# A graph network's edge passes: single rows fetched from ScalarE's DMA queue instead of SyncE's

## The chip, the cores and the metric

The kernel runs on one core of one Trainium2 chip. A core has five engines with instruction streams of their own: TensorE (PE), VectorE (DVE), ScalarE (ACT), GpSimd (POOL) and SyncE (SP), which computes nothing and issues DMAs. Sixteen DMA engines move the data. The metric is the device time of one execution in microseconds (us), lower is better; the kernel before takes 6624.49 us (median of 3 runs, 6611.32 to 6628.42).

## The reference, cut to what matters

Two graph layers over 12500 nodes of 128 features and 200000 edges, sorted by their destination. The first is attention with 8 heads, the second a plain sum over the neighbours:

```python
q, k, v = (h @ W + b for each of Wq, Wk, Wv)       # 12500 x 128
e = sum(q[dst] * k[src]) / 4                       # per edge and head
p = exp(e - segment_max(e, dst)[dst]); z = segment_sum(p, dst)
agg = segment_sum((p / z[dst]) * v[src], dst)
...                                                # projection, norm, MLP
neigh = segment_sum(h2[src], dst)                  # second layer
out = x + relu((h2 + neigh) @ W1 + b1) @ W2 + b2
```

(The self loops of the first layer, the norms and the residuals are left out here.) The costly part is `k[src]`, `v[src]` and `h2[src]`: 200000 rows at addresses that only the edge list tells.

## The kernel before, in words

The work goes in stages, named by the letters of the functions: A (node projections, search of where each node's edges start), B (first edge pass, from about 400 to 3300 us of the span), C (nodes: attention output and MLP), D (second edge pass, about 3640 to 6430 us) and E (nodes: last MLP).

**Edges.** Each of the 128 partitions owns 1568 consecutive edges, which are walked in 98 batches of 16 per partition. A running maximum and running sums go along the free axis by VectorE's scans, and each edge's running state is stored to memory.

**Gathers.** For a batch n, GpSimd issues 16 indirect DMAs (helper at L698), each of which fetches one row for each of the 128 partitions: keys and values (1 KB) into `kvb[n % 2]` in pass B, `h2` rows (512 B) into `rows[n % 2]` in pass D. A buffer is free again once batch n - 2 is consumed (`weighed_s` in B, `rows_turned` in D).

**Single rows.** Both passes are written in octets of 8 batches (`octets`, L511): the first octet is peeled with fixed addresses, 11 are a hardware loop (`Fori`), and two batches are left. In every octet's slot 1, from the second octet on, the last of the 16 indirect DMAs is left out. Its 128 rows are instead fetched one by one by ordinary DMAs of one row each (`fetch`, DMAs at L594): SyncE loads their numbers into registers (`row_numbers`, two register loads at L587: a pointer, then the values), computes an address and issues the DMA. The 128 rows of the next octet are spread over the slots of this one: `ROWS_B` = 0, 8, then 20 in each of six slots; `ROWS_D` = 19, 19, then 18 in each of five, then 0. They land in `direct_kv` or `direct_h`, and one DMA of SyncE (L614 in B, L664 in D) copies them into their place in the batch's buffer (`direct_set` counts these copies).

**SyncE's other work.** In B, one load of 1 MB of queries per batch (L603, `q_in`), issued when ScalarE has turned earlier queries (`q_turned`), and one store of states of 1.15 MB (L580, after `stb_set`, counted in `states_out`). In D one store of sums per batch (L655, after `sums_set`, counted in `sums_out`). All of it is in one program order with the single rows.

**ScalarE in B** (`batch_b`, from L1115), per batch n: the gates and keep factors of batch n + 1 (L1097, L1099, L1103); wait for the queries and for VectorE's products (`prod_s`); keep the last query (L1126), turn the queries of batch n + 1 (two copies, L1108); exponential (L1131); then copies of top, z and both halves of the states into the buffer that is stored (L1135, L1138, two at L1142), each after VectorE's scan that makes it. **VectorE in B** multiplies and reduces (L1739, L1746), waits for the turned queries (L1680), scans for the maxima and sums (L1770 to L1832) and ends with the second scan of the states (L1810).

**ScalarE in D** (`slot_d`, from L1235), per batch: wait for the rows, turn them (L1247), indices and keep factors (L1248, L1231), wait for the store of two batches before (`sums_out`), then two copies of sums (L1254) after VectorE's two scans (L1994).

Of the kernel before, what the change touches and what calls it, by code (L numbers as in the profile page):

```python
# [55 lines left out]
EREST = E - EFULL * STEPS  # L56
OCTETS = BATCHES // 8
DIRECT_AT = 9 * B + B - 1
ROWS_B = (0, 8) + (20,) * 6
ROWS_D = (19, 19) + (18,) * 5 + (0,)  # L60
assert BATCHES == 8 * OCTETS + 2 and sum(ROWS_B) == P and sum(ROWS_D) == P
BPAIRS = BATCHES // 2
# [70 lines left out]
def build(nc, a, out):  # L133
    ctx = ExitStack()
    with ctx:
# [385 lines left out]
        def settle(eng):  # L521


            eng.sem_inc(turns, 1)

        def last_batch(n):
            return isinstance(n, int) and n == BATCHES - 1
# [8 lines left out]
        def _(sp):  # L536
# [42 lines left out]
                settle(sp)  # L579
                sp.dma_start(by_step(states0)[:, bass.ds(n * B, B), :], stb[k]).then_inc(states_out[k], 16)  # L580

            def row_numbers(o, by_slot, r):

                if not by_slot[r]:
                    return []
                p0 = sum(by_slot[0:r])
                return nc.values_load_multi_w_load_instructions(  # L587
                    direct_tab[bass.ds(o, 1), p0:p0 + by_slot[r]], engines=[mybir.EngineType.SP], min_val=0, max_val=N - 1,
                    skip_runtime_bounds_check_because="edges name nodes")[1]

            def fetch(to, tab, numbers, p0, done):

                for p, number in enumerate(numbers, p0):
                    sp.dma_start(to[p:p + 1, :], tab[bass.ds(number, 1), :]).then_inc(done, 16)  # L594

            def slot_b(o, r, first):

                n, k = o * 8 + r, r % 2
                if not last_batch(n):
                    if not (first and r == 0):  # L600
                        sp.wait_ge(q_turned, n * 2)
                        settle(sp)
                    sp.dma_start(qb[1 - k], q_rows[:, bass.ds(n * B + B, B), :]).then_inc(q_in[1 - k], 16)  # L603
                filling = not (isinstance(o, int) and o == OCTETS)
                numbers = row_numbers(o, ROWS_B, r) if filling else []
                p0, ahead = sum(ROWS_B[0:r]), len(numbers) // 2 if r > 1 else 0
                fetch(direct_kv, kv_tab, numbers[0:ahead], p0, direct_kv_in)
                if not (first and r == 0):
                    store_b(n - 1, 1 - k)
                if r == 0 and not first:  # L610
                    sp.wait_ge(direct_kv_in, o * 16 * P)
                    sp.wait_ge(weighed_s, n * 2)
                    settle(sp)
                    sp.dma_start(kvb[1][:, B - 1, :], direct_kv).then_inc(direct_set, 16)  # L614
                if r == 1 and not first and filling:
                    sp.wait_ge(direct_set, o * 16)
                    settle(sp)
                fetch(direct_kv, kv_tab, numbers[ahead:], p0 + ahead, direct_kv_in)
            sp.wait_ge(direct_listed, 16)
            octets(sp, slot_b)  # L620


# [25 lines left out]
            def slot_d(o, r, first):  # L648

                n, k = o * 8 + r, r % 2  # L650
                filling = not (isinstance(o, int) and o == OCTETS)
                numbers = row_numbers(o, ROWS_D, r) if filling else []
                sp.wait_ge(sums_set, n + 1)
                settle(sp)
                sp.dma_start(by_step(states1)[:, bass.ds(n * B, B), :], sums_b[k]).then_inc(sums_out[k], 16)  # L655
                if r == 0 and not first and filling:
                    sp.wait_ge(direct_set, (OCTETS + o) * 16)
                    settle(sp)
                fetch(direct_h, h2_tab, numbers, sum(ROWS_D[0:r]), direct_h_in)
                if r == 7:  # L660
                    sp.wait_ge(direct_h_in, o * 16 * P + 16 * P)
                    sp.wait_ge(rows_turned, n + 1)
                    settle(sp)
                    sp.dma_start(rows[1][:, B - 1, :], direct_h).then_inc(direct_set, 16)  # L664
# [364 lines left out]
        def _(act):  # L1029
# [66 lines left out]
            def gates(n, k):  # L1096
                nc.scalar.copy(keepz[k].rearrange("p (h t) -> p h t", h=NH)[:, :, 1:CW],  # L1097
                               keep[:, bass.ds(n * B, B)].unsqueeze(1).to_broadcast([P, NH, B])).then_inc(gates_set, 1)
                nc.scalar.copy(penb[k][:, 0:NH * CW].rearrange("p (h t) -> p h t", h=NH)[:, :, 1:CW],  # L1099
                               pen[:, bass.ds(n * B, B)].unsqueeze(1).to_broadcast([P, NH, B])).then_inc(gates_set, 1)  # L1100
# [12 lines left out]
            act.wait_ge(q_in[0], 16)  # L1113
            turn_queries(0)

            def batch_b(i, first):
                for k in range(2):
                    n = i * 2 + k
                    gates(n + 1, 1 - k)
                    keep_features(n + 1, 1 - k)  # L1120
                    if not last_batch(n):
                        act.wait_ge(q_in[1 - k], i * 16 + 16 + (16 if k else 0))
                        settle(act)
                        act.wait_ge(prod_s, (n + 1) * 2)
                        settle(act)
                        nc.scalar.copy(q_last, q_now[:, :, B - 1])  # L1126
                        act.drain()
                        turn_queries(1 - k)
                        nc.scalar.copy(idx[k][:], src_all[:, bass.ds((n + 2) * B, B)]).then_inc(idx_set, 1)
                    act.wait_ge(dif_s, n + 1)  # L1130
                    nc.scalar.activation(probs, dif.rearrange("p h t -> p (h t)"), ACT.Exp, scale=SCALE)\  # L1131
                        .then_inc(probs_s, 1)
                    if not first:
                        act.wait_ge(states_out[k], i * 16)
                    nc.scalar.copy(stb[k][:, :, SW:RW].rearrange("p b h -> p h b"), top[:, :, 1:CW])\  # L1135
                        .then_inc(top_out, 1)
                    act.wait_ge(zrun_s, n + 1)
                    nc.scalar.copy(stb[k][:, :, HID:SW].rearrange("p b h -> p h b"),  # L1138
                                   zrun[k].rearrange("p (h t) -> p h t", h=NH)[:, :, 1:CW]).then_inc(z_out, 1)
                    for half in range(2):  # L1140
                        act.wait_ge(state_s, n * 2 + half + 1)
                        done = nc.scalar.copy(stb[k][:, :, half * HF:(half + 1) * HF].rearrange("p b f -> p f b"),  # L1142
                                              sums_flat[:, half * HF * B:(half + 1) * HF * B].rearrange("p (f b) -> p f b", b=B))
                        if half == 0 and last_batch(n):
                            act.wait_ge(chunk_s, 4)
                            nc.scalar.activation(weight, masked, ACT.Exp, scale=SCALE).then_inc(chunk_act, 1)
                    done.then_inc(stb_set, 1)
            repeat(act, BPAIRS, batch_b, tail=1)


            act.wait_ge(chunk_ps, 2)
# [82 lines left out]
            def slot_d(o, r, first):  # L1234

                n, k = o * 8 + r, r % 2
                act.wait_ge(rows_in[k], o * (4 * BW - 16 * k) + r // 2 * BW + BW)
                if r == 1 and not first:
                    act.wait_ge(direct_set, (OCTETS + o) * 16)
                act.wait_ge(sum_s, n * 2 + 1)  # L1240
                if last_batch(n):
                    for half in range(2):
                        fs = slice(half * HF, (half + 1) * HF)
                        nc.scalar.copy(rows_now[:, fs, :], rows[k][:, :, fs].rearrange("p b f -> p f b"))\
                            .then_inc(rows_turned, 1)
                else:
                    nc.scalar.copy(rows_now, rows[k].rearrange("p b f -> p f b")).then_inc(rows_turned, 1)  # L1247
                    nc.scalar.copy(idx[k][:], src_all[:, bass.ds((n + 2) * B, B)]).then_inc(idx1_set, 1)  # L1248
                    keep1_features(n + 1, 1 - k)
                if not (first and r < 2):  # L1250
                    act.wait_ge(sums_out[k], o * 64 + r // 2 * 16)
                for half in range(2):
                    act.wait_ge(sum_s, n * 2 + half + 2)
                    done = nc.scalar.copy(sums_b[k][:, :, half * HF:(half + 1) * HF].rearrange("p b f -> p f b"),  # L1254
                                          run_sums[:, half * HF * B:(half + 1) * HF * B].rearrange("p (f b) -> p f b", b=B))
                done.then_inc(sums_set, 1)
            octets(act, slot_d)
            act.wait_ge(carry1_ps, 1)
            nc.scalar.copy(sameT, ps[:, 0, 0:P]).then_inc(sameT_s, 1)  # L1259
# [805 lines left out]
```

## Time and profile before

| | |
|---|---|
| median of 3 runs | 6624.49 us |
| span of the profiled execution | 6623.6 us |
| pass B, pass D (about) | 400 to 3300 us, 3640 to 6430 us |
| busy: POOL, DVE, ACT, PE | 3391.3, 2759.1, 2126.7, 517.3 us |
| DMA packets of SyncE's queue (q1) | 87088, 462.32 MB |
| DMA packets of ScalarE's queue (q10) | 14722, 13.70 MB |
| DMA packets of GpSimd's queue (q0) | 142272, 342.22 MB |

The span is the time from the first to the last instruction of one profiled execution. An engine's busy time counts its own work only: instructions for registers, branches, semaphores and the issuing of DMAs are not in it, and SyncE has no busy time at all. What an engine's sequencer does is seen in the rows whose engine name ends in q (SPq, ACTq). No engine is busy in more than about half of the span, so the order of the waits decides, and the chain of waits and the timeline have to be read.

### The profile page before, as it was taken

To read this page: it belongs to the slowest core of one execution; us is meant where nothing else is said; L and a number is where in the kernel's file an instruction comes from. 1 tells how busy PE (TensorE), PEld (TensorE's weight loads), DVE (VectorE), ACT (ScalarE), POOL (GpSimd) and SP (SyncE) were. 2 spreads that over 40 slices of the span, in tenths; PEclk is the share of its full clock that TensorE was granted. 3 is DMA by queue.
4 is the path that set the end of the run, shared out by engine and by line. 5 is a ranking of instruction groups with operands and counts; after the bars stand their busy time and mean duration, and the time that the engine had idled before them with its cause. 6 is when DMAs were issued, how large, how long until landed. Compare 5 with 4: busy or idle time off the path is not lost.

```text
span 6623.6 us, 31560 instructions
## 1 busy us (share of the span) xinstructions
PE 517.3 (8%) x2379; PEld 363.4 (5%) x2379; DVE 2759.1 (42%) x4388; ACT 2126.7 (32%) x2237; POOL 3391.3 (51%) x3586
## 2 busy tenths in 40 slices
PE   4400000000000000000076000000000000000006
PEld 2200000000000000000055000000000000000004
DVE  7556666566565566666665121112111111212112
ACT  3223333233333333333355332223232322323221
POOL 4665555455355455554353564645455454545534
PEclk8655555555555555555588555555555555555557
DMA  9954444444444444444344222222222222222223
GB/s 362 372 185 159 138 154 153 132 150 147 133 155 135 151 142 149 159 135 151 128 104 97 65 80 78 68 71 83 65 78 73 75 65 71 85 66 77 71 80 106
DMA packets 244283, 819.95 MB, mean 124 GB/s; under 512 B 70090, under 2 KB 103030, under 8 KB 193907
## 3 DMA queue, kind: packets, MB, share of 16 engines
q0 software_dynamic: 142272, 342.22, 19.0%
q1 hardware_dynamic: 87088, 462.32, 18.6%
q10 hardware_dynamic: 14722, 13.70, 0.6%
q14 instruction: 193, 1.57, 0.1%
q8 instruction: 8, 0.13, 0.0%
HBM read 455.00 MB, written 354.21 MB: 122 GB/s over the span
## 4 chain that ended last, share of the span: by engine, by line
SPq 47%; issue 35%; DVE 5%; PE 4%; DMA 3%; ACT 2%; POOL 2%; another core or an unknown queue 1%; POOLq 0%; ACTq 0%; DVEq 0%
SPq L594 31%; SPq L587 12%; DVE arena L1810 2%; DMA q_edges<-arena 2%; PE ps L1372 1%; PE ps L1361 1%; DVE ps L1687 1%; DMA arena<-q_edges 1%; SPq L580 1%; POOL q_edges L702 1%; SPq L655 1%; DVE ps L1793 1%; ACT ps L1108 1%; POOL arena L698 1%
## 5 line engine op out<-in xcount | busy, mean ns | idle before, releaser
L698 POOL DMA_INDIRECT arena<-kv_tab,idx x1556 | 1475.3, 948 | 1425.3 <-DVE ps L1793 926.2
L698 POOL DMA_INDIRECT arena<-h_tab,idx x1556 | 1472.0, 946 | 1302.4 <-ACT idx L1248 807.9
L1986 DVE SCALAR_TENSOR_TENSOR ps<-arena,keep,ps 128x128 f32<-128x128 f32 x97 | 42.5, 438 | 2297.5 <-ACT ps L1247 1947.1
L1254 ACT COPY arena<-arena 128x1024 f32<-128x1024 f32 x196 | 364.2, 1925 | 1714.0 <-DMA states<-arena 1651.4
L1142 ACT COPY arena<-arena 128x1024 f32<-128x1024 f32 x196 | 377.7, 1927 | 557.7 <-DVE arena L1810 474.0
L1687 DVE TENSOR_TENSOR_SCAN ps<-arena,ps 128x256 f32<-128x256 f32 (+2 forms) x584 | 502.6, 861 | 1.0 <-remote 0.9
L1680 DVE SCALAR_TENSOR_TENSOR ps<-arena,keep,ps 128x64 f32<-128x64 f32 x194 | 53.6, 276 | 1062.9 <-ACT ps L1108 1026.0
L1810 DVE TENSOR_TENSOR_SCAN arena<-arena,ps 128x1024 f32<-128x1024 f32 x196 | 443.4, 2262 | 6.0 <-remote 3.1
L1247 ACT COPY ps<-arena 128x2048 f32<-128x2048 f32 x97 | 346.8, 3576 | 284.7 <-DMA arena<-arena 153.3
L1994 DVE TENSOR_TENSOR_SCAN arena<-arena,ps 128x1024 f32<-128x1024 f32 x194 | 433.1, 2274 | 10.3 <-issue 0.5
L1108 ACT COPY ps<-arena 128x1024 f32<-128x1024 f32 x196 | 362.1, 1880 | 10.2 <-DMA arena<-q_edges 4.1
L1126 ACT COPY arena<-ps 128x128 f32<-128x128 f32 x97 | 25.5, 263 | 1009.4 <-DMA arena<-q_edges 996.5
L698 POOL DMA_INDIRECT arena<-states,node_idx x196 | 191.3, 976 | 152.8 <-issue 64.6
L1739 DVE TENSOR_TENSOR arena<-arena,ps 128x1024 f32<-128x1024 f32 x196 | 229.0, 1210 | 21.8 <-DMA arena<-kv_tab,idx 18.5
L1793 DVE TENSOR_TENSOR ps<-arena,ps 128x1024 f32<-128x1024 f32 x196 | 237.3, 1211 | 0.0
L1332 PE MATMUL ps<-arena,ones 128*128 128x512 f32 x4 | 3.8, 1101 | 2936.6 <-DVE arena L1713 2936.6
L1746 DVE TENSOR_REDUCE ps<-arena 128x64 f32<-128x1024 f32 x196 | 230.2, 1220 | 0.1
L1407 PE MATMUL ps<-arena 128*128 128x128 f32 x2 | 0.8, 501 | 2820.6 <-ACT arena L1259 2820.6
L1332 PEld LDWEIGHTS ps<-arena,ones 128*128 128x128 f32 x4 | 1.2, 324 | 2938.1 <-DVE arena L1713 2937.1
L1407 PEld LDWEIGHTS ps<-arena 128*128 128x128 f32 x2 | 0.5, 310 | 2820.8 <-ACT arena L1259 2820.8
L698 POOL DMA_INDIRECT arena<-dst_tab,idx x98 | 97.5, 995 | 103.1 <-DVE idx L1604 68.9
L702 POOL DMA_INDIRECT q_edges<-arena,start_i x98 | 101.6, 1037 | 39.7 <-issue 31.8
(252 smaller groups left out, 2510.0 us busy)
## 6 DMA issues: line engine op xcount, KB each, us to landing
states<-arena SPq DMA_DIRECT2D x98, 1152.0 KB
q_edges<-arena SPq DMA_DIRECT2D x98, 1024.0 KB
arena<-q_edges SPq DMA_DIRECT2D x98, 1024.0 KB
states<-arena SPq DMA_DIRECT2D x98, 1024.0 KB
arena<-kv_tab,idx POOLq DMA_INDIRECT x1556
arena<-h_tab,idx POOLq DMA_INDIRECT x1556
arena<-kv_tab SPq DMA_DIRECT2D x1536, 1.0 KB
arena<-h_tab SPq DMA_DIRECT2D x1536, 0.5 KB
```

What stands on the lines that cost most here:

```text
L587: return nc.values_load_multi_w_load_instructions(direct_tab[bass.ds(o, 1), p0:p0 + by_slot[r]], engines=[mybir.EngineType.SP], min_val=0, ...
L594: sp.dma_start(to[p:p + 1, :], tab[bass.ds(number, 1), :]).then_inc(done, 16)
L698: pool.indirect_dma_start(to, None, tab, bass.IndirectOffsetOnAxis(ap=at, axis=0)).then_inc(done, 16)
L1108: nc.scalar.copy(q_now[:, fs, :], qb[k][:, :, fs].rearrange("p b f -> p f b")).then_inc(q_turned, 1)
L1142: done = nc.scalar.copy(stb[k][:, :, half * HF:(half + 1) * HF].rearrange("p b f -> p f b"), sums_flat[:, half * HF * B:(half + 1) * HF * ...
L1247: nc.scalar.copy(rows_now, rows[k].rearrange("p b f -> p f b")).then_inc(rows_turned, 1)
L1254: done = nc.scalar.copy(sums_b[k][:, :, half * HF:(half + 1) * HF].rearrange("p b f -> p f b"), run_sums[:, half * HF * B:(half + 1) * HF ...
L1687: done = nc.vector.tensor_tensor_scan(part, keep_flat[n % 2][:, 0:(f1 - f0) * B], part, 0.0, ALU.mult, ALU.add)
L1746: nc.vector.tensor_reduce(score[:, :, 1 + b0:1 + b1].rearrange("p h t -> p t h"), kvb[n % 2][:, b0:b1, 0:HID].rearrange("p b (h d) -> p b ...
L1793: nc.vector.tensor_tensor(weighed.rearrange("p (h d) b -> p b h d", d=HD), values.rearrange("p b (h d) -> p b h d", d=HD), probs_h[:, half ...
L1810: nc.vector.tensor_tensor_scan(sums_flat[:, half * HF * B:(half + 1) * HF * B], keep_flat[n % 2], weighed_flat, 0.0, ALU.mult, ALU.add).th ...
L1994: nc.vector.tensor_tensor_scan(run_sums[:, part], keep1_flat[n % 2], rows_flat[:, part], 0.0, ALU.mult, ALU.add).then_inc(sum_s, 1)
```

## The change

ScalarE's instruction stream issues the single rows of both passes. SyncE keeps the loads of queries, the stores and the copy into place, with their waits on `direct_kv_in` and `direct_h_in`. In B the fetch of a slot stands after the gates and keep factors and before the wait for the queries; in D it stands at the end of the slot, after the second copy of the sums. ScalarE waits for `direct_set` before it overwrites the landing buffer (slot 1 in B, end of slot 0 in D) and once for `direct_listed`. `ROWS_B` is now 0, 14, then 19 six times. ScalarE's pass B becomes a loop over octets instead of one over pairs of batches. GpSimd's, VectorE's and TensorE's streams stay as they are.

```diff
-ROWS_B = (0, 8) + (20,) * 6
+ROWS_B = (0, 14) + (19,) * 6
@@ SyncE, pass B: slot_b
-                filling = not (isinstance(o, int) and o == OCTETS)
-                numbers = row_numbers(o, ROWS_B, r) if filling else []
-                p0, ahead = sum(ROWS_B[0:r]), len(numbers) // 2 if r > 1 else 0
-                fetch(direct_kv, kv_tab, numbers[0:ahead], p0, direct_kv_in)
                 if not (first and r == 0):
                     store_b(n - 1, 1 - k)
...
-                if r == 1 and not first and filling:
-                    sp.wait_ge(direct_set, o * 16)
-                    settle(sp)
-                fetch(direct_kv, kv_tab, numbers[ahead:], p0 + ahead, direct_kv_in)
-            sp.wait_ge(direct_listed, 16)
@@ SyncE, pass D: slot_d
-                numbers = row_numbers(o, ROWS_D, r) if filling else []
...
-                if r == 0 and not first and filling:
-                    sp.wait_ge(direct_set, (OCTETS + o) * 16)
-                    settle(sp)
-                fetch(direct_h, h2_tab, numbers, sum(ROWS_D[0:r]), direct_h_in)
@@ ScalarE, pass B
+            def row_numbers(o, by_slot, r):
+                if not by_slot[r]:
+                    return []
+                p0 = sum(by_slot[0:r])
+                return nc.values_load_multi_w_load_instructions(
+                    direct_tab[bass.ds(o, 1), p0:p0 + by_slot[r]], engines=[mybir.EngineType.Activation], min_val=0, max_val=N - 1,
+                    skip_runtime_bounds_check_because="edges name nodes")[1]
+            def fetch(to, tab, numbers, p0, done):
+                for p, number in enumerate(numbers, p0):
+                    act.dma_start(to[p:p + 1, :], tab[bass.ds(number, 1), :]).then_inc(done, 16)
+            def slot_b(o, r, first):
+                n, k = o * 8 + r, r % 2
+                i = o * 4 + r // 2
+                gates(n + 1, 1 - k)
+                keep_features(n + 1, 1 - k)
+                if r == 1 and not first and filling(o):
+                    act.wait_ge(direct_set, o * 16)
+                    settle(act)
+                if filling(o):
+                    fetch(direct_kv, kv_tab, row_numbers(o, ROWS_B, r), sum(ROWS_B[0:r]), direct_kv_in)
+                if not last_batch(n):
+                    act.wait_ge(q_in[1 - k], i * 16 + 16 + (16 if k else 0))
...
+            act.wait_ge(direct_listed, 16)
+            octets(act, slot_b)
@@ ScalarE, pass D: end of slot_d
                 done.then_inc(sums_set, 1)
+                if r == 0 and not first and filling(o):
+                    act.wait_ge(direct_set, (OCTETS + o) * 16)
+                    settle(act)
+                if filling(o):
+                    fetch(direct_h, h2_tab, row_numbers(o, ROWS_D, r), sum(ROWS_D[0:r]), direct_h_in)
```

## Rows read from the trace of the kernel before

**Rows 1.** The page's chain that ended last: share of the span by engine and line.

```profile
SPq 47%; issue 35%; DVE 5%; PE 4%; DMA 3%; ACT 2%; POOL 2%; another core or an unknown queue 1%; POOLq 0%; ACTq 0%; DVEq 0%
SPq L594 31%; SPq L587 12%; DVE arena L1810 2%; DMA q_edges<-arena 2%; PE ps L1372 1%; PE ps L1361 1%; DVE ps L1687 1%; DMA arena<-q_edges 1%; SPq L580 1%; POOL q_edges L702 1%; SPq L655 1%; DVE ps L1793 1%; ACT ps L1108 1%; POOL arena L698 1%
```

**Rows 2.** SyncE's timeline in pass B: start us, us from first to last of the group, engine.

```profile
2012.44 3.90 SPq L594 DMA_DIRECT2D arena<-kv_tab  x10
...
2022.98 0.36 SPq L603 DMA_DIRECT2D arena<-q_edges  x1
2028.97 4.60 SPq L594 DMA_DIRECT2D arena<-kv_tab  x10
...
2035.05 30.96 SPq L594 DMA_DIRECT2D arena<-kv_tab  x10
2070.99 0.36 SPq L603 DMA_DIRECT2D arena<-q_edges  x1
```

**Rows 3.** Timeline of pass B around it: GpSimd, ScalarE, VectorE; [idle before <-releaser].

```profile
2025.51 0.95 POOL L698 DMA_INDIRECT arena<-kv_tab,idx  x1 [22.09 <-DVE ps L1793]
...
2064.27 0.94 POOL L698 DMA_INDIRECT arena<-kv_tab,idx  x1 [0.30 <-issue]
...
2096.37 0.26 ACT L1126 COPY arena<-ps 128x128 f32<-128x128 f32 x1
...
2112.35 1.94 ACT L1142 COPY arena<-arena 128x1024 f32<-128x1024 f32 x1 [3.85 <-issue]
...
2115.37 0.27 ACT L1126 COPY arena<-ps 128x128 f32<-128x128 f32 x1
```

**Rows 4.** Source views of L614 and L664: instructions, ns min/median/max, first to last start.

```profile
L614 SPq DMA_DIRECT2D arena<-arena x12: 18/522/527, 636.3 to 3259.2; - x12
L664 SPq DMA_DIRECT2D arena<-arena x12: 520/533/698, 3907.1 to 6418.0; - x12
```

**Rows 5.** Source views of the loop branch L515: same columns.

```profile
L515 SPq ALU_OP  x22: 2/56/698, 860.2 to 6418.6; - x22
L515 ACTq ALU_OP  x11: 35/35/35, 4093.6 to 6394.2; - x11
```

**Rows 6.** Source views of L594, L587, L1103, L1086: registers, loads and single DMAs.

```profile
L594 SPq DMA_DIRECT2D arena<-kv_tab x1536: 1/228/1407, 428.3 to 3251.0; - x192
...
L587 SPq TENSOR_LOAD <-direct_tab x168: 3/2850/8149, 399.2 to 6400.2; - x168
L587 SPq TENSOR_LOAD <-direct_tab_ptr x154: 13/1188/4003, 637.5 to 6398.9; - x154
...
L1103 ACTq FUSED_REGOPS  x94: 52/52/58, 455.7 to 3214.0; - x94
...
L1086 ACTq DMA_DIRECT2D last_tab<-arena x1: 477/477/477, 347.3 to 347.3; - x1
```

**Rows 7.** Source view of L1031: a store of 128 partitions by ScalarE.

```profile
L1031 ACTq DMA_DIRECT2D dst_tab<-arena x1: 360/360/360, 17.8 to 17.8; - x1
```

**Rows 8.** ScalarE's timeline in stage A, a copy and a DMA behind it in its program.

```profile
314.54 0.94 ACT L1055 COPY arena<-arena 128x896 f32<-128x896 f32 x1 [11.96 <-issue]
314.56 0.54 ACTq L1036 DMA_DIRECT2D kv_tab<-arena  x1
```

**Rows 9.** Timeline of pass D: ScalarE and SyncE over a slot with all rows there.

```profile
4356.92 0.53 SPq L664 DMA_DIRECT2D arena<-arena  x1
4361.00 3.59 ACT L1247 COPY ps<-arena 128x2048 f32<-128x2048 f32 x1 [14.14 <-DMA arena<-arena]
...
4371.46 3.57 ACT L1247 COPY ps<-arena 128x2048 f32<-128x2048 f32 x1
...
4380.53 1.92 ACT L1254 COPY arena<-arena 128x1024 f32<-128x1024 f32 x1 [0.23 <-issue]
```

**Rows 10.** Windows of pass B and pass D: busy us (instructions), clock, DMA share, GB/s.

```profile
406.00:3260.00 2854.00, 0.00 (x0) 0.00 (x0) 1754.09 (x2403) 972.10 (x1154) 1445.95 (x1526) 0.50 0.44 146
3642.00:6398.00 2756.00, 0.00 (x0) 0.00 (x0) 470.64 (x288) 786.68 (x481) 1455.97 (x1540) 0.50 0.24 73
```

More of the change, by code:

```diff
@@ L580, in store_b @@
                 sp.dma_start(by_step(states0)[:, bass.ds(n * B, B), :], stb[k]).then_inc(states_out[k], 16)
[L582 to L594, printed above, removed]
             def slot_b(o, r, first):
@@ L650, in slot_d @@
                 n, k = o * 8 + r, r % 2
-                filling = not (isinstance(o, int) and o == OCTETS)
-                numbers = row_numbers(o, ROWS_D, r) if filling else []
                 sp.wait_ge(sums_set, n + 1)
@@ L1114, in _ @@
             turn_queries(0)
[L1116 to L1147, printed above, removed]
@@ L1148, in _ @@
-            repeat(act, BPAIRS, batch_b, tail=1)
+            def row_numbers(o, by_slot, r):
[8 more added lines that the diff above has]
+                    act.dma_start(to[p:p + 1, :], tab[bass.ds(number, 1), :]).then_inc(done, 16)
@@ new lines, in filling @@
+            def filling(o):
+                return not (isinstance(o, int) and o == OCTETS)
+            def slot_b(o, r, first):
[11 more added lines that the diff above has]
+                    settle(act)
+                    act.wait_ge(prod_s, (n + 1) * 2)
+                    settle(act)
+                    nc.scalar.copy(q_last, q_now[:, :, B - 1])
+                    act.drain()
+                    turn_queries(1 - k)
+                    nc.scalar.copy(idx[k][:], src_all[:, bass.ds((n + 2) * B, B)]).then_inc(idx_set, 1)
+                act.wait_ge(dif_s, n + 1)
+                nc.scalar.activation(probs, dif.rearrange("p h t -> p (h t)"), ACT.Exp, scale=SCALE)\
+                    .then_inc(probs_s, 1)
+                if not (first and r < 2):
+                    act.wait_ge(states_out[k], i * 16)
+                nc.scalar.copy(stb[k][:, :, SW:RW].rearrange("p b h -> p h b"), top[:, :, 1:CW])\
+                    .then_inc(top_out, 1)
+                act.wait_ge(zrun_s, n + 1)
+                nc.scalar.copy(stb[k][:, :, HID:SW].rearrange("p b h -> p h b"),
+                               zrun[k].rearrange("p (h t) -> p h t", h=NH)[:, :, 1:CW]).then_inc(z_out, 1)
+                for half in range(2):
+                    act.wait_ge(state_s, n * 2 + half + 1)
+                    done = nc.scalar.copy(stb[k][:, :, half * HF:(half + 1) * HF].rearrange("p b f -> p f b"),
+                                          sums_flat[:, half * HF * B:(half + 1) * HF * B].rearrange("p (f b) -> p f b", b=B))
+                    if half == 0 and last_batch(n):
+                        act.wait_ge(chunk_s, 4)
+                        nc.scalar.activation(weight, masked, ACT.Exp, scale=SCALE).then_inc(chunk_act, 1)
+                done.then_inc(stb_set, 1)
@@ L1256, in slot_d @@
                 done.then_inc(sums_set, 1)
+                if r == 0 and not first and filling(o):
+                    act.wait_ge(direct_set, (OCTETS + o) * 16)
+                    settle(act)
+                if filling(o):
+                    fetch(direct_h, h2_tab, row_numbers(o, ROWS_D, r), sum(ROWS_D[0:r]), direct_h_in)
             octets(act, slot_d)
```

## The prediction

> **What bounds the kernel now.** The page's chain of waits comes first [rows 1]: 31% of the span is SyncE at L594, the DMAs of single rows and the register instructions of each, 12% is SyncE's register loads at L587, and much of the 35% "issue" lies between such instructions. No working engine has more than 5%. So SyncE's instruction stream sets the end, mostly in B and D.
>
> The timeline of SyncE says why [rows 2]. It issues ten rows in 3.90 us at one time, (3.90 - 0.22) / 9 = 0.41 us a row, and in 30.96 us a little later, 3.1 us a row. The engines' timeline beside it [rows 3] shows GpSimd's gathers from 2025.51 to 2064.27. The ten rows from 2028.97 still take only 4.60 us; those from 2035.05 are slow, and the slow stretch ends just after the gathers. So while gathers are in flight, from some 8 us after their start, SyncE crawls. It isn't the DMA instruction alone: SyncE's loop arithmetic at L515 has a median of 56 ns and a maximum of 698, while ScalarE's at the same line has 35/35/35 [rows 5], and ScalarE's register instruction at L1103 in B never took more than 58 ns in 94 times [rows 6], although these fell among gathers too. ScalarE's sequencer does not crawl.
>
> An octet takes (3259.2 - 636.3) / 11 = 238.4 us in B and (6418.0 - 3907.1) / 11 = 228.3 us in D, by the copies into place, one in each [rows 4]. What else could bound it: GpSimd needs (2064.27 - 2025.51) / 30 = 1.29 us a gather over 31 gathers in a row [rows 3], 127 x 1.29 = 164 us an octet. ScalarE and VectorE hand over to each other in a chain of 19.0 us a batch in B when nothing is late (2115.37 - 2096.37 [rows 3]), 152 us an octet; in D of 10.5 us (4371.46 - 4361.00 [rows 9]). SyncE holds up some 74 us an octet in B and 64 in D.
>
> **What the change removes.** SyncE's 128 rows, their register instructions and 14 register loads (seven slots, two each) per octet and pass leave SyncE. What stays per batch is one load and one store in B, one store in D. At the crawl, five instructions of 0.7 us each are some 4 us, and a slot has at least 10. SyncE is off the path, and the 74 and 64 us are open.
>
> **What it adds.** The same instructions on ScalarE, which is in the chain.
> - Register loads: on SyncE the medians are 2.85 us for the values and 1.19 for the pointer [rows 6], 4.2 with the arithmetic between them. In B the stretch from the end of the load of queries to the first row was 2028.97 - 2023.34 = 5.6 us [rows 2]. I take 5.6 in B and 4.2 in D. Bounds: 3.0 (1.19 and a short load of values) to 8.1 + 1.2 = 9.3, the slowest load of values beside a median pointer.
> - One row: at least SyncE's 0.41. ScalarE's plain store of 128 partitions takes 360 ns to issue [rows 7], SyncE's load of 128 partitions 0.36 [rows 2], so ScalarE's issuing costs the same; its register instruction (52 ns) is a little longer. I take 0.44. From above: ScalarE's only DMA of one element took 477 ns against 228 for SyncE's row [rows 6], which makes 0.66.
> - Hidden part in B: the fetch stands behind the copy at L1142 and three short copies. ScalarE's sequencer runs ahead of its copies: the DMA of [rows 8] is behind the copy in the program and starts 0.02 us after it starts. So the loads begin about 0.7 us after the copy that starts at 2112.35 [rows 3], at 2113.1, and 2115.37 - 2113.1 = 2.3 us of them are hidden. The rest is in the chain, since VectorE goes no further in a batch before the next queries are turned.
> - B, octet: slot 0 has 19.0; slot 1 19.0 - 2.3 + 5.6 + 14 x 0.44 = 28.5; six slots 19.0 - 2.3 + 5.6 + 19 x 0.44 = 30.7 each, 184. Sum 231.7. Gathers (20.6 us a batch) are hidden in such slots: two buffers, and two neighbouring slots have 47 us or more.
> - D, octet: the last copy of a slot starts 4380.53 - 4371.46 = 9.07 us after its rows are turned [rows 9], and the fetch goes out beside that copy. Slots 0 and 1: 9.1 + 4.2 + 19 x 0.44 = 21.7; five slots with 18 rows 21.2; slot 7 without any 10.5. Sum 159.9, just under the gathers' 164. Both are nearly the bound; I take 165.
> - Loop end: ScalarE's loop is now eight slots with 128 rows. SyncE, whose loop has such a size, has 2070.99 - 2066.01 = 5.0 us between its last row and the next octet's load, the crawl included [rows 2]. Bounds 0 to 5; I take 2 in B (in D it is within the 165).
>
> Of this last term the Trainium skill says more (Runtime: NRT & Kernel Launch, Instruction fetch mechanics): a taken branch to a target outside the two-page window waits for a fetch of the page. ScalarE's loop would then pay at each of 22 loop ends; without the rule the time would be 22 us less. No row shows it alone.
>
> **New waits.** ScalarE waits for `direct_set` in slot 1 of B and at the end of slot 0 of D. Queued behind it are the fetch, the turning of the queries and all the slot's copies, and VectorE waits for these. The copy into place is issued when the octet's slot 0 begins, or slot 7 in D has turned its rows, and takes 4361.00 - 4356.92 = 4.1 us to land [rows 9]; ScalarE comes some 12 us or more later. Nothing for it. The wait for `direct_listed` is over long before.
>
> **Sum.** B: 238.4 - 233.7 = 4.7 us gained in each of 11 octets, 52; the first, with fixed addresses and without the pointer load, is about even. D: 228.3 - 165 = 63.3, in 12 octets 760. Together 812: 6623.6 - 812 = 5812 of the profiled span, which is the median of the runs (6624.5) within 1 us. Forecast 5810.
>
> **The forecast's own range.** Low end: 0.41 a row, loads of 3.0: B 19.0 + 25.4 + 6 x 27.5 = 209.4, 348 less; D at gathers of 1.25 us, 160, 820 less: 5460. High end: loads and rows between my value and the upper bounds, 6100.
>
> **Rivals.**
> 1. *ScalarE's issue is dear.* At 0.66 a row B is 19.0 + 31.5 + 6 x 34.8 + 2 = 262, 24 more, x 12 = 285 lost; D 2 x 25.8 + 5 x 25.2 + 10.5 + 2 = 190, 38 less, 459 gained: 6450. For it: the 477 ns. Against it: that DMA is not a row, and the 360 ns. Each 0.01 us a row is 31 us over 3072 rows, so the break-even is near 0.72 a row.
> 2. *The crawl moves with the rows* (the slower side). If what slows SyncE is the state of the DMA engines' queues for small DMAs during gathers, ScalarE's rows cost 3.1 us too. Each slot has a batch of gathers in flight for 20 us, some 17 of them crawling: 5.5 rows in these, 13.5 rows after them in 5.9 us, so a fetch is 28.5 us in B and 27.1 in D. Octets: B 19.0 + 43 + 6 x 45.2 + 2 = 335, D 7 x 36.2 + 12.5 = 266; (97 + 38) x 12 = 1610 more: 8230. It decides as soon as ScalarE's rows exceed 0.72 us on average. For it: all gathers and rows share the DMA engines. Against it: their share is 0.44 in B and 0.24 in D [rows 10]; instructions that touch no DMA crawl on SyncE too [rows 5]; and ScalarE's DMA of [rows 8], in a run of gathers, took its 0.54 us.
> 3. *Nothing is gained:* SyncE's stores and loads at the crawl, or the gathers, keep both octets where they are, within 0.3% of 6624. Against it: the gathers' floor is 164.
>
> Beside the second stands the Trainium skill (DMA: Bandwidth & Descriptors, Issuing engines are not separate DMA queues): DMAs started by the scalar, sync or gpsimd engine run on the same 16 DMA engines and interleave. By that rule the transfers gain nothing and only the issuing is relieved; were the rows slow in the transfer, the rival's 8230 would stand, and if in the issuing, the forecast. The trace agrees with issuing, as register instructions of 0.7 us do not wait for a transfer.
>
> **Chances.** Forecast 0.60, rival 1 0.18 (nearly all of it faster), rival 2 0.15, rival 3 0.03, and 0.04 for gains of other size. Range 5460 to 6500, which takes in rival 1 and leaves out the second. Faster by over 0.3% (about what a measurement of this kernel can tell from no change): 0.80; within it 0.03; slower 0.17.
>
> **What would show it.** In the trace after: rows on ACTq at about 0.44 us, among gathers too; the single-row lines out of the chain; gaps between ScalarE's starts at the copy of the last query of about 19, 28 and 31 us in B; in D GpSimd issuing almost without a pause and octets of 165 us. Wrong if ACTq's rows take over 0.7 us, if its register loads take 5 us or more each, or if D's octet stays above 190.

## The result, and the profile after

The changed kernel took 6814.78 us (median of 4 runs, 6789.32 to 6823.18) where the kernel before took 6618.03 (4 runs): a ratio of 1.030, 95% interval 1.027 to 1.033. The forecast was 5810 with a range of 5460 to 6500. The pair was timed again in three later sessions (a session is a set of kernels timed on one chip beside the kernel before). The ratio was 1.031 (1.026 to 1.036) and 1.034 (1.026 to 1.041); in the third, with 2 runs of the changed kernel, 1.020 (1.011 to 1.030).

One thing has to be known for every number below: one and the same kernel runs in one of two settings, and all kernels of a session were in the same one. In the first measurement and in three sessions the kernel before took 6547 to 6652 us, and an engine that issues rows crawls at times, as [rows 2] show ("with the crawl"). In two sessions it took 4761 us and nothing crawled. One chip was found in either setting at different times. What sets it was not found. Ratios are taken within a session only.

The chain of waits of the kernel after (share of the span by engine, then by line; L1092 is ScalarE's register loads, L1099 its rows), against [rows 1]:

```profile
issue 28%; DVE 26%; ACTq 25%; ACT 11%; PE 5%; another core or an unknown queue 2%; POOL 1%; DMA 1%; SPq 0%; DVEq 0%; POOLq 0%
ACTq L1099 16%; ACTq L1092 9%; DVE arena L1810 6%; DVE arena L1994 6%; ACT ps L1242 5%; DVE ps L1687 4%; DVE ps L1793 3%; ACT ps L1079 2%; PE ps L1372 1%; ACT arena L1249 1%; ACT arena L1074 1%; PE ps L1316 1%; PE ps L1361 1%; POOL arena L669 1%
```

SyncE is out of the chain, as forecast, and ScalarE's sequencer has come in, with 25%. The source views of the two copies into place, L596 in B and L635 in D, give the octets as [rows 4] did before (times in ns, then the first and the last start):

```profile
L596 SPq DMA_DIRECT2D arena<-arena x12: 471/482/550, 687.3 to 3712.8; - x12
```

```profile
L635 SPq DMA_DIRECT2D arena<-arena x12: 63/85/515, 4325.3 to 6610.3; - x12
```

B has (3712.8 - 687.3) / 11 = 275.0 us an octet, D (6610.3 - 4325.3) / 11 = 207.7. Against 238.4 and 228.3 that is 36.6 more and 20.6 less, and (36.6 - 20.6) x 12 = 192 of the 198 us by which the span grew. Both passes missed: 234 and 165 were forecast. (The first measurement and all profiles in this section have the crawl.)

One slot of B in the timeline after (start us, us, engine, line), to hold against [rows 3]:

```profile
2010.22 0.27 ACT L1120 COPY arena<-ps 128x128 f32<-128x128 f32 x1 [18.61 <-issue]
...
2026.19 1.94 ACT L1136 COPY arena<-arena 128x1024 f32<-128x1024 f32 x1 [3.85 <-DVE arena L1810]
...
2040.12 8.15 ACTq L1099 DMA_DIRECT2D arena<-kv_tab  x19
2048.60 0.27 ACT L1120 COPY arena<-ps 128x128 f32<-128x128 f32 x1 [19.28 <-issue]
```

The rows begin only at 2040.12, 13.9 us after the copy, where 0.7 + 5.6 were forecast. The source view of L1092 in that slot, then in two later ones, says where the time is (TENSOR_LOAD of `direct_tab` is the load of values, ns):

```profile
L1092 ACTq TENSOR_LOAD <-direct_tab_ptr x1: 1160/1160/1160, 2026.8 to 2026.8; - x1
...
L1092 ACTq TENSOR_LOAD <-direct_tab x1: 11852/11852/11852, 2028.1 to 2028.1; - x1
```

```profile
L1092 ACTq TENSOR_LOAD <-direct_tab x1: 3232/3232/3232, 2194.3 to 2194.3; - x1
```

```profile
L1092 ACTq TENSOR_LOAD <-direct_tab x1: 2986/2986/2986, 5055.5 to 5055.5; - x1
```

The first reads 19 values and takes 11.85 us. The second, in a slot of the octet after, also reads 19 and takes 3.23; the third, in D, reads 18 in 2.99, where its neighbour takes 7.58. What divides them is the number in the list at which a slot begins, the sum of the shares before it. Median of 12 loads each, in us:

| first number | 0 | 14 | 33 | 52 | 71 | 90 | 109 | D: 0 | 19 | 38 | 56 | 74 | 92 | 110 |
|---|---|---|---|---|---|---|---|---|---|---|---|---|---|---|
| values read | 14 | 19 | 19 | 19 | 19 | 19 | 19 | 19 | 19 | 18 | 18 | 18 | 18 | 18 |
| after, ScalarE | 2.40 | 12.1 | 12.2 | 3.25 | 12.1 | 12.2 | 12.2 | 3.31 | 8.22 | 7.70 | 2.77 | 7.76 | 2.74 | 7.74 |
| before, SyncE | | | | | | | | 3.13 | 5.30 | 7.67 | 2.79 | 7.58 | 2.86 | 7.71 |

Where the first number is a multiple of four the load is short. The kernel before had B's loads at 0, 8, 28, 48, 68, 88 and 108, all short (medians 1.7 to 2.6 us); D had four long ones out of seven even then. The new `ROWS_B` is what made five of B's long.

The rows themselves, the source view of L1099 (ns):

```profile
L1099 ACTq FUSED_REGOPS  x3072: 1/37/1397, 431.5 to 6597.6; - x192
...
L1099 ACTq DMA_DIRECT2D arena<-h_tab x1536: 1/217/767, 4120.2 to 6598.4; - x192
```

A row is cheap on ScalarE: the median from start to start is 0.37 us, less than SyncE's 0.41. But register instructions of up to 1.4 us stand among them: ScalarE crawls too. The time from a fetch's first row to its last, divided by its rows, has a mean of 0.65 us in D and 0.45 in B. Two slots of D show it:

```profile
4970.36 22.08 ACTq L1099 DMA_DIRECT2D arena<-h_tab  x19
...
5058.62 13.84 ACTq L1099 DMA_DIRECT2D arena<-h_tab  x18
5072.62 3.59 ACT L1242 COPY ps<-arena 128x2048 f32<-128x2048 f32 x1 [16.44 <-issue]
```

At 0.37 us, 18 rows take 6.5 us; here they take 13.84, and the next batch waits for them. The first fetch, of 19 rows, belongs to slot 0 of its octet and takes 22.08.

### The profile page after: what moved, and what is told of

Its sections match the earlier page's. It is cut to its first block, busy times and chain, and to the rows that moved or that the text cites. A ratio compares the mean times of both kernels' runs of the same rounds, so it can differ in the third digit from the quotient of the medians.

```text
span 6821.4 us, 31442 instructions
## 1 busy us (share of the span) xinstructions
PE 521.7 (8%) x2379; PEld 366.7 (5%) x2379; DVE 2753.6 (40%) x4388; ACT 2161.6 (32%) x2237; POOL 3389.9 (50%) x3586
## 4 chain that ended last, share of the span: by engine, by line
issue 28%; DVE 26%; ACTq 25%; ACT 11%; PE 5%; another core or an unknown queue 2%; POOL 1%; DMA 1%; SPq 0%; DVEq 0%; POOLq 0%
ACTq L1099 16%; ACTq L1092 9%; DVE arena L1810 6%; DVE arena L1994 6%; ACT ps L1242 5%; DVE ps L1687 4%; DVE ps L1793 3%; ACT ps L1079 2%; PE ps L1372 1%; ACT arena L1249 1%; ACT arena L1074 1%; PE ps L1316 1%; PE ps L1361 1%; POOL arena L669 1%
## 5 line engine op out<-in xcount | busy, mean ns | idle before, releaser
L1136 ACT COPY arena<-arena 128x1024 f32<-128x1024 f32 x196 | 378.6, 1932 | 550.6 <-DVE arena L1810 536.4
L1249 ACT COPY arena<-arena 128x1024 f32<-128x1024 f32 x196 | 379.1, 1934 | 212.5 <-DVE arena L1994 206.1
```

## The experiments

Theory A: a load of values is long where it does not start at a multiple of four, and such loads, in the chain, cost the time. Theory B: loads are slow because of the traffic beside them. What the crawl is came second.

**Aligned shares on ScalarE.**

```diff
-ROWS_B = (0, 14) + (19,) * 6
-ROWS_D = (19, 19) + (18,) * 5 + (0,)
+ROWS_B = (0, 8) + (20,) * 6
+ROWS_D = (20,) * 4 + (16,) * 3 + (0,)
```

> The changed kernel with other shares of rows per slot alone: ROWS_B 0, 8, then 20 six times; ROWS_D 20 four times, 16 three times, 0, so that every register load starts at a number divisible by four. Theory A (a register load of values that starts elsewhere reads them one by one, 12.1 us in B and 7.7 in D, and 2.3 to 3.3 us where it starts at a multiple of four): all loads of values fall to about 2.4 us; B's octet 275 - 49 = 226 us, D's 208 - 25 = 183; total 6815 - 12 x 74 = 5930 us. Theory B (loads are slow because ScalarE makes them while gathers and the 1 MB transfers are in flight, wherever they start): loads stay at 8 to 12 us and the time stays within 1% of the changed kernel's 6815. A mixed result: loads are short but the rows, now issued sooner after the gathers begin, meet more of the crawl (over 0.7 us each): 6100 to 6400.

> The changed kernel with loads at multiples of four alone. Without the crawl 5470 as before. With the crawl, by the sum of the two halves measured apart (B on ScalarE 255 us an octet, D on ScalarE 205): 4761 is not its measure but 12 x (255 + 205) + the rest, 6862 - 12 x (21 + 4.6) = 6555 us.

The first, in a session without the crawl: 5469.68 us beside 4761.46, ratio 1.148 (1.146 to 1.150). The second, in a session with it: 6535.22 beside 6584.36, 0.991 (0.988 to 0.995), where 6555 was expected from the two halves below. The source views, two lines of the first run and one of the second:

```profile
L1092 ACTq TENSOR_LOAD <-direct_tab x168: 1145/2418/2861, 411.9 to 5262.0; - x168
```

```profile
L1099 ACTq FUSED_REGOPS  x3072: 37/37/53, 413.2 to 5271.0; - x192
```

```profile
L1092 ACTq TENSOR_LOAD <-direct_tab x168: 1111/2358/2809, 425.5 to 6300.7; - x168
```

No load is longer than 2.9 us now, in either setting, and theory B is out: engine, place and traffic are the same. The absolute forecast (5930) missed, since it was made for a kernel before of 6618. Without the crawl B's octet is 219 us and D's 160, where the kernel before has 160 in both (below), so the loss of 15% sits in B. In the session with the crawl the change itself took 6817.14 and this form 6535.22: aligned shares alone are worth 282 us there and turn a loss of 3.4% into a gain of 0.9%. B's octet goes from 276 to 257 us, D's from 209 to 204. The loads became 49 us an octet shorter in B, and 19 us came out: the rows now crawl more. By the measure used above they take 0.65 us each in B instead of 0.45, and 0.81 in D instead of 0.65; without the crawl the same kernel has 0.41 in both passes.

**Aligned shares on SyncE**, the kernel before with this `ROWS_D` alone.

> The kernel before (rows on SyncE) with ROWS_D 20 four times, 16 three times, 0 alone. Theory A: in D four loads per octet fall from 5.3 to 7.7 us to about 2.5, some 19 us of an octet of SyncE's path: 6618 - 230 = 6390 us. Theory B: no load changes, 6618 within 0.3%. If SyncE's crawl during gathers takes the freed time back: 6450 to 6618.

> The kernel before with D's loads at multiples of four. Without the crawl 4761, the same as the kernel before. With it: D's octet falls from 229 to 213 as in the run that had B's rows on ScalarE and D's on SyncE: 6620 - 12 x 15 = 6440 us.

Without the crawl: 4760.64, ratio 1.000 (0.999 to 1.001). With it, in a later session: 6426.42 beside 6547.46, 0.978 (0.970 to 0.985), as theory A says for that setting (6440 was expected then). D's octet is 214 us, against 228 in the first measurement. The chain of waits of the run without the crawl:

```profile
POOL 56%; issue 25%; DMA 9%; PE 5%; DVE 3%; ACT 2%; SPq 0%; POOLq 0%; ACTq 0%; DVEq 0%
```

and its source views of rows and of the loop branch:

```profile
L594 SPq FUSED_REGOPS  x3072: 37/37/47, 412.3 to 4556.7; - x192
```

```profile
L515 SPq ALU_OP  x22: 48/57/66, 695.2 to 4570.7; - x22
```

Without the crawl SyncE issues the same rows in step with the gathers, GpSimd is the bound, and an octet takes 159.8 us in B and 159.4 in D. There the kernel before has nothing to gain from SyncE's relief.

**The changed shares on SyncE**, the kernel before with `ROWS_B = (0, 14) + (19,) * 6` alone.

> The kernel before with the changed kernel's ROWS_B (0, 14, then 19 six times) alone, rows still on SyncE. Theory A: five loads of values per octet in B go from 2.4 to 8 or 12 us, 28 to 48 us more on SyncE's path: 6618 + 340 to 580 = 6960 to 7200 us. Theory B: no load changes, 6618 within 0.5%.

4839.91 beside 4761.46, 1.017 (1.015 to 1.018), without the crawl. The loads follow theory A: a slot that starts at 90 has

```profile
L587 SPq TENSOR_LOAD <-direct_tab x1: 9206/9206/9206, 1001.9 to 1001.9; - x1
```

and the median of five slots is 8.7 us, of the slot at 52 3.9. Five loads are some 6 us longer each, but only 6.4 us an octet came out in the time (B's octet is 166.2 us): SyncE's stream had slack. So the long load comes with the shares on either engine, and its price depends on the slack of the stream that it stands in.

**Fixed rows on ScalarE.** The 128 rows have constant addresses, rows 0 to 127 of the table whatever the edges say: no loads, one instruction a row.

```diff
-                return nc.values_load_multi_w_load_instructions(
...
+                return list(range(p0, p0 + by_slot[r]))
...
-                    act.dma_start(to[p:p + 1, :], tab[bass.ds(number, 1), :]).then_inc(done, 16)
+                    act.dma_start(to[p:p + 1, :], tab[number:number + 1, :]).then_inc(done, 16)
```

> The aligned form of the changed kernel with rows at fixed addresses: no register loads, no address arithmetic, one DMA instruction per row on ScalarE (the rows fetched are always rows 0 to 127 of the table, so this part of the computation is left out). It prices all of the loads and the registers' share of the crawl. Theory A: B's octet 226 - 7 x 3.5 - 128 x 0.1 = 189 us, D's at the gathers' bound near 165: 5930 - 12 x 55 = 5270 us. If the crawl hangs on the number of DMAs and not of instructions, rows still take up to 3 us during gathers and it stays above 5500.

5079.21 beside 4761.46, 1.067 (1.064 to 1.069); 5081.64 in a second session, both without the crawl, so that this run could not price the registers' share of the crawl. B has 186.4 us an octet, D 159.3. So of the aligned form's 59 us over the gathers' 160 in B, 33 are loads and register instructions, 27 the DMAs' own issuing. D reaches the gathers' bound, as the aligned form does (159.9).

**The change again.**

> The changed kernel itself, timed beside the kernel before in the setting where SyncE does not crawl and the kernel before takes 4761 us (in the first measurement it took 6618, with the crawl). Theory A (the change puts register loads and rows into the chain of ScalarE and VectorE; crawl or not): B's gaps 38 us where a load of values starts off a multiple of four, octet about 260 us; D's octet 190 to 200 us: 4761 + 12 x (260 - 160) + 12 x (195 - 159) = 6390 us, ratio 1.3 or more. Theory C (the change's cost is the crawl that went over to ScalarE): without a crawl it is near the kernel before, under 5000. If the crawl is back in this call, the kernel before is near 6618 again and the changed one near 6815.

6862.20 beside 6652.11, 1.031: the crawl was back. The change itself was never met without the crawl, also not in two later sessions (6817.14 beside 6584.36, and 6700.91 beside 6547.46, where 6815 to 6862 was expected), so that its cost there stays open; the 6390 expected here, later 6170, was not tested.

**One pass at a time** (aligned shares; B's rows on SyncE and D's on ScalarE, and the reverse).

In the first of the two, SyncE's `slot_b` has its fetches of the kernel before again, and ScalarE's `slot_b` loses them; the second does the same with `slot_d`, `ROWS_D` and `direct_h`:

```diff
+                fetch(direct_kv, kv_tab, numbers[0:ahead], p0, direct_kv_in)
...
+                fetch(direct_kv, kv_tab, numbers[ahead:], p0 + ahead, direct_kv_in)
...
-                if filling(o):
-                    fetch(direct_kv, kv_tab, row_numbers(o, ROWS_B, r), sum(ROWS_B[0:r]), direct_kv_in)
```

> B's rows on SyncE as in the kernel before, D's rows on ScalarE, all loads starting at multiples of four. Theory A: B at the gathers' 160 us, D's 159.6: the same as the kernel before within 0.5% (4761 to 4785) without the crawl. With the crawl, B 238 and D about 175 to 185: 6618 - 12 x 50 = 6020.

> B's rows on ScalarE, D's on SyncE, all loads starting at multiples of four. Theory A: all of the loss of the aligned form sits in B: 5470 within 0.5% without the crawl (ratio 1.148). If D on ScalarE cost anything, it is below 5450. With the crawl, 6618 - 12 x 12 - 12 x 19 = 6250.

Both in one session with the crawl, the kernel before at 6652.11: D alone on ScalarE 6326.30, 0.952 (0.947 to 0.957); B alone on ScalarE 6696.87, 1.007 (1.004 to 1.009). Octets by pass: B 240.2 on SyncE and 255.2 on ScalarE; D 213.4 on SyncE and 204.7 on ScalarE. D gained less than expected (6020) and B cost more (6250): in both, the engine that has the rows crawls.

**Rows in ScalarE's idle gaps.** Aligned; in B the loads stand before the wait for the running sums, six rows before the first copy of the states, the rest between its halves.

```diff
+                numbers = row_numbers(o, ROWS_B, r) if filling(o) else []
                 act.wait_ge(zrun_s, n + 1)
...
+                fetch(direct_kv, kv_tab, numbers[0:6], p0, direct_kv_in)
                 for half in range(2):
...
+                    if half == 0:
+                        fetch(direct_kv, kv_tab, numbers[6:], p0 + 6, direct_kv_in)
```

> The aligned form with B's fetch moved out of the chain: the register loads stand before the wait for the running sums (2.3 us idle before that copy), six rows before the first copy of the states (1.8 us idle), the other rows between its two halves (3.85 us idle and 1.9 us of a copy that the sequencer runs ahead of). Theory A (place in the chain is the cost, not ScalarE as such): a batch takes 19.5 to 21 us, so B is at the gathers' 160 to 168 us an octet and the time 4761 to 4860 without the crawl. Theory D (ScalarE's sequencer pays for 20 rows and two loads wherever they stand): 28 us a batch, 5470. With the crawl: between 5000 and 5900, below the kernel before.

6387.88 beside 6652.11, 0.960 (0.956 to 0.965), where 5000 to 5900 was expected; in another session 6293.53 beside 6547.46, 0.958 (0.948 to 0.969). Both had the crawl, so the question of the place without it stays open. B's octet is 241 us, 14 less than in the chain; it is also what SyncE's own takes in that session, 240. In the other session the two are 235.7 (gaps) and 235.8 (SyncE). So outside the chain ScalarE's crawl costs B as much as SyncE's.

**Rows divided over both engines.** Aligned; SyncE 12 of 20 (8 of 16 in D), ScalarE 8, in the gaps.

```diff
+SYNC_B = (0, 8) + (12,) * 6
+SYNC_D = (12,) * 4 + (8,) * 3 + (0,)
...
+                    fetch(sp, direct_kv, kv_tab, row_numbers(SYNC, o, p0, SYNC_B[r]), p0, direct_kv_in)
...
+                p0 = sum(ROWS_B[0:r]) + SYNC_B[r]
+                numbers = row_numbers(SCALAR, o, p0, ROWS_B[r] - SYNC_B[r]) if filling(o) else []
```

> The rows of each slot are divided: in B SyncE fetches 8 in slot 1 and 12 of 20 in the others, ScalarE 8 of 20 (loads before the wait for the running sums, 4 rows before the first copy of the states, 4 between its halves); in D SyncE 12 of 20 or 8 of 16, ScalarE 8; all loads start at multiples of four. Theory E (the crawl is a budget of each sequencer: while gathers are in flight an engine can issue only so many instructions before each of them takes 0.7 us, so that it is the number of instructions per engine that counts): neither engine exceeds it for long, B falls from 240 to 165 to 195 us an octet and D from 229 to 165 to 180: 6620 - 12 x 100 = 5400 us (5000 to 5800). Theory F (one budget shared by both queues, as rows of both go through the same DMA engines): B stays near 240, D near 205, 6300 to 6400 as in the two runs before. Where the setting of this call has no crawl: 4761 to 4800, as the kernel before.

Of its second run, beside the change once more:

> Rows divided over SyncE and ScalarE. It took 4762 without the crawl, as the kernel before. With the crawl: theory E (a budget of instructions per sequencer) 5000 to 5800; theory F (one budget for both) 6300 to 6400. Without it: 4762 again.

4762.50 beside 4761.76 without the crawl, 1.000 (0.999 to 1.001). With it 6159.84 beside 6584.36, 0.936 (0.928 to 0.943): octets of 234 and 194 us. Of the kernels that fetch the rows named by the edges it is the fastest, and it costs nothing in the other setting. Neither theory of the recorded text fits: one budget of instructions shared by both engines was to give 6300 to 6400, one for each engine 5000 to 5800. Its timeline (SyncE and ScalarE, rows L545) has both crawl together:

```profile
1606.49 32.92 SPq L545 DMA_DIRECT2D arena<-kv_tab  x9
...
1614.19 14.00 ACTq L545 DMA_DIRECT2D arena<-kv_tab  x4
```

SyncE takes 32.92 / 9 = 3.7 us a row and ScalarE 14.00 / 4 = 3.5, at once. ScalarE's other instructions crawl with its rows now. The register instruction of its wait before each half of the states (L1152) has:

```profile
L1152 ACTq ALU_OP  x165: 3/38/722, 635.1 to 3192.6; - x165
```

It takes over 0.6 us in 50 of 165 times. In the kernel before no register instruction of ScalarE does.

**Fixed rows on SyncE**, the same edit in the kernel before with aligned `ROWS_D`, in a session without the crawl (4762.76 beside 4761.76) and in one with it:

> SyncE with rows at fixed addresses: one instruction a row instead of three, no register loads (rows 0 to 127 are fetched whatever the edges say, so this part of the computation is left out). With the crawl: if it counts instructions, 4800 to 5300; if it counts row DMAs, 6300 to 6620. Without it 4762 again.

5476.06 beside 6584.36, 0.831 (0.822 to 0.839). There are as many DMAs as before, a third of the instructions for each row, and no register loads. The octets are 188 and 182, against 238 and 228 in the first measurement and 160 without the crawl. Instructions are most of what the crawl charges, but not all, as 5300 was the upper end of that theory. Not separated is that these DMAs always read the same 128 rows.

## Why the prediction was wrong

- *SyncE bounds the kernel, at the crawl:* right, and so was its relief; it is out of the chain. Right in this setting alone: 4761 us without the crawl could not be read from the trace.
- *The crawl is SyncE's own ("ScalarE's sequencer does not crawl"):* wrong, the step that failed first. The aligned form shows what it cost. Its loads are shorter than the forecast's, and with the crawl it still takes 6535 us, with octets of 257 and 204; without the crawl the same kernel has 219 and 160, not far from the low end of the forecast's own sum (209 and 160, with loads of 3.0 us). The difference, (38 + 44) x 12, is nearly 1000 us, as much as the forecast missed by. [Rows 5] and [rows 6] showed ScalarE's register instructions at 35 and 52 ns among gathers, but ScalarE issued no rows then. After the change its loop arithmetic at L515 is still 35/35/35, while its register instructions between rows reach 1.4 us, so that row never tested the question. The DMA of [rows 8] was a single one.
- *Rival 2* had the mechanism, and 8230 was too high for it: it charged 3.1 us for every row within 17 us of gathers. The fetches behind long loads crawl less. From row to row (mean of a fetch, median of a slot's 12 fetches) they have 0.41 or 0.42 us in B and 0.45 to 0.56 in D. Behind short loads it is 0.66 in B's slot of number 52, and 0.77, 0.78 and 1.26 in D; only the 14 rows of B's slot 1 have 0.43. Why a fetch that starts late is spared is not shown.
- *Loads of 5.6 us in B and 4.2 in D:* the second step, a mis-sized term. The two loads measured 13.2 us in five of seven slots of B (bound given: 9.3), and 8.7 to 9.3 in four of seven of D. The shares of rows were taken as a change of size only; that their sums decide how a load runs was in the trace of before, in D, hidden in one line with a median of 2.85 and a maximum of 8.1 us [rows 6].
- *0.44 us a row:* right where nothing crawls (0.37 is the median, 0.41 the mean by the measure above); with the crawl 0.45 in B and 0.65 in D. 0.21 x 128 = 27 us of D's 43 us miss is this, and the loads are 19. Rival 1, a dear issue by ScalarE itself, is out: its row is cheaper than SyncE's.
- *19.0 us of chain, and what of the fetch is hidden:* right. The slot above has 2048.60 - 2010.22 = 38.4 us; 19.0 + 1.2 + 11.9 + 8.2 + 0.5 between them - 2.4 hidden = 38.4.
- *Sum by the octet:* B is 41 us over the forecast. Five slots take 38.2 us instead of 30.7, which is 38 us and is the loads (13.2 instead of 5.6). The slot of number 52 takes 35 instead of 30.7 although its load is short, because its rows crawl; slot 1 is 1.4 us shorter than forecast. The two failed steps are not to be added: short loads bring more crawl, as the aligned form shows.
- *Issuing and not transfer:* the Trainium skill (DMA: Bandwidth & Descriptors, Issuing engines are not separate DMA queues) says that DMAs of several issuing engines share the 16 DMA engines, so that only the time to issue is saved. The runs agree: 5476 us with as many transfers of the same size says that most of the crawl's cost is in the instructions.
- *New waits:* they cost nothing, as forecast; `direct_set` is no releaser in the chain of the changed kernel.
- *Loop end, 2 us in B:* the stall is there. ScalarE's branch itself is short, but its next instruction starts 2.4 us later:

```profile
L515 ACTq COMPARE_BRANCH  x1: 50/50/50, 2064.6 to 2064.6; - x1
L515 ACTq FUSED_REGOPS  x1: 78/78/78, 2067.1 to 2067.1; - x1
```

This gap is 2.4 to 2.7 us at all 20 branches that are taken (the last branch of each loop is not), where ScalarE's loop of pass D in the kernel before has 0.11 us. From the last query's copy in slot 7 to the next one it is 21.9 us (median) with such a branch between, and 19.0 in the two octets without one. So the loop end costs 2.9 us an octet in B; in D it is 11.4 against 10.5, or 0.9. The prediction counted 22 loop ends for both passes.

What stays open: what puts a chip into the setting with the crawl, what exactly it counts, and why a long load takes 12.1 us in B (ScalarE, with the crawl), 8.7 in B (SyncE, without it) and 7.7 in D in both.

## What to carry to other kernels

When a change alters shares or offsets "only" in passing, look at each group of the affected instruction by its offset before trusting a median: bimodal durations in one line have a cause. That an engine is spared an effect is shown only where it does what the afflicted engine does. And work for a queue that stands in the chain goes into its idle gaps, or is divided; in the chain nearly its whole length is added (19.4 of 21.8 us in the slot above). A branch's own record doesn't show what it costs: look at when the next instruction starts.

## What the runs showed of the hardware

- A register load of 18 to 20 numbers takes 2.3 to 3.3 us where the first is a multiple of four in a row of 4-byte numbers (up to 3.9 on SyncE in B), and 7.6 to 12.2 us elsewhere: 20 values 2.4, 19 3.25, 18 2.8, and 16 2.0 us when aligned; 18 values 7.7 and 19 8.2 when not, 0.43 us a value. So when aligned, four more values (16 to 20) cost about as much as one more (18 to 19). On SyncE and ScalarE alike.
- ScalarE issues a one-row DMA with its register work every 0.37 us (0.30 with a constant address), SyncE every 0.41; medians where nothing crawls.
- After a loop branch that is taken, ScalarE starts its next instruction 2.4 to 2.9 us later where the loop has 509 or 600 recorded instructions (but for one of 0.4), and within 0.2 us where it has 95 to 225. Between them the size doesn't decide: 0.2 us with 293 and 356, 2.4 with 316.
- With one and the same program, sequencers that issue many small DMAs among gathers either keep their pace (0.37 to 0.41 us a row, 4761 us) or fall to some 0.7 us an instruction (6547 to 6652 us), depending on when it is run; two engines crawl at once.
